# Attention over 32 graphs: xT loaded a batch ahead, keys in natural order, squares loaded in four transfers

## What is computed

```
q = x @ Wq.T ; k = x @ Wk.T ; v = x @ Wv.T + bv          # split into 12 heads
a = einsum('bnhd,bmhd->bhnm', q, k) * 384**-0.5 + adj[:, None]
a = where(all(a == 0, axis=-1), -inf, a) ; a = nan_to_num(softmax(a))
o = einsum('bhnm,bmhd->bnhd', a, v).reshape(B, N, 384)
y = layernorm(x + o @ Wo.T + bo)
```

## Time and profile before

| | |
|---|---|
| median of three runs | 781.46 us (780.7 to 782.91) |
| the profiled execution | 779.59 us, its span 777.70 us |
| busy: PE, DVE, ACT, POOL | 93%, 77%, 79%, 58% of the span |
| mean granted clock of TensorE | 0.97 |
| transfers | 193 MB, 71.0% of 16 engines' span in the one queue of SP |
| squares: stores and loads | 64 each, 1024 KB each |
| xt, xr, out | 32 each, 384 KB each |
| bias_sq, bias | 32 each, 256 KB each |

### The profile page before, as it was taken

The page is one execution under the profiler, slowest core; times in us unless marked ns, Lnnn a source line. Parts: engine busy times, 40 slices in busy tenths (PEclk is TensorE's granted clock), DMA queues, the critical chain, the costliest instruction groups (busy, mean ns, idle before and its releaser), DMA issues.

```text
span 777.7 us, 22949 instructions
## 1 busy us (share of the span) xinstructions
PE 722.7 (93%) x7480; PEld 613.3 (79%) x7480; DVE 594.9 (77%) x2216; ACT 615.1 (79%) x1991; POOL 453.2 (58%) x518
## 2 busy tenths in 40 slices
PE   7788999999999899999999999999999999998753
PEld 6777888888888788888888888888888888876632
DVE  2776887888887788888788888888788888878821
ACT  2786888888888788898888888988889889878711
POOL 3425666765666676656666756566667665665321
PEclk8999999999999999999999999999999999999955
DMA  8187768778777876878768778786787777776621
GB/s 256 55 283 233 257 236 283 246 262 299 253 259 235 278 260 249 301 263 280 261 244 294 259 246 294 264 284 231 268 290 268 249 286 270 247 279 233 248 81 42
DMA packets 92664, 193.00 MB, mean 248 GB/s; under 512 B 4736, under 2 KB 51584, under 8 KB 84352
## 3 DMA queue, kind: packets, MB, share of 16 engines
q1 hardware_dynamic: 92544, 191.52, 71.0%
HBM read 111.80 MB, written 79.69 MB: 246 GB/s over the span
## 4 chain that ended last, share of the span: by engine, by line
PE 61%; DMA 18%; POOL 7%; ACT 5%; issue 4%; DVE 2%; SPq 1%; POOLq 0%; ACTq 0%; DVEq 0%
PE bank_b L532 35%; DMA xt<-in_xT 14%; PE bank_a L619 8%; PE s_bank L578 7%; PE bank_t L589 6%; POOL xt_lo L323 4%; PE bank_c L532 4%; ACT prob L437 3%; PE bank_c L600 2%; POOL xt_hi L321 2%; ACT y_out L468 2%; DMA sq_dram<-w_f 2%; DVE neg L782 1%; DMA xr<-in_x 1%; SPq L259 1%
## 5 line engine op out<-in xcount | busy, mean ns | idle before, releaser
L437 ACT ACTIVATE prob<-neg,negmax 128x256 f32<-128x256 f32 x768 | 380.8, 501 | 37.6 <-DVE negmax L782 35.1
L782 DVE CUSTOM_DVE_ANT_0 neg<-s_bank,bias_sq 128x256 f32<-128x256 f32 x512 | 191.0, 410 | 47.0 <-PE s_bank L578 46.1
L796 DVE STREAM_TRANSPOSE w_f<-prob 128x512 f32<-128x512 f32 x256 | 173.1, 695 | 0.0
L437 ACT ACTIVATION_READ_ACCUMULATOR prob<-neg,negmax 128x1 f32 x768 | 148.1, 193 | 0.0
L532 PE MATMUL bank_b<-xt_hi,w_hi 128*128 128x256 f32 x384 | 117.1, 305 | 20.1 <-POOL xt_lo L323 16.4
L334 POOL TENSOR_TENSOR kq_lo<-kq,kq_hi 128x512 fp32r<-128x512 f32 x96 | 124.0, 1291 | 7.7
L532 PE MATMUL bank_b<-xt_lo,w_hi 128*128 128x256 f32 x384 | 110.7, 288 | 0.0
L532 PE MATMUL bank_b<-xt_hi,w_lo 128*128 128x256 f32 x384 | 110.4, 288 | 0.0
L782 DVE CUSTOM_DVE_ANT_0 neg<-s_bank,bias 128x256 f32<-128x256 f32 x256 | 92.3, 416 | 10.6 <-PE s_bank L578 10.5
L532 PEld LDWEIGHTS bank_b<-xt_hi,w_hi 128*128 128x128 f32 x384 | 75.1, 196 | 30.1 <-issue 20.0
L360 POOL TENSOR_SCALAR var_eps<-meanvar 128x2 f32<-128x2 f32 x32 | 7.3, 227 | 151.4 <-DVE meanvar L880 151.4
(11 more groups left out here) (66 smaller groups left out, 1835.6 us busy)
## 6 DMA issues: line engine op xcount, KB each, us to landing
sq_dram<-w_f SPq DMA_DIRECT2D x64, 1024.0 KB, 5.9
sq_probT<-sq_dram SPq DMA_DIRECT2D x64, 1024.0 KB, 5.9
xt<-in_xT SPq DMA_DIRECT2D x32, 384.0 KB, 5.9
xr<-in_x SPq DMA_DIRECT2D x32, 384.0 KB, 4.6
out_y<-y_out SPq DMA_DIRECT2D x32, 384.0 KB, 5.1
bias_sq<-in_adjP SPq DMA_DIRECT2D x32, 256.0 KB, 6.2
bias<-in_adj SPq DMA_DIRECT2D x32, 256.0 KB, 6.1
w_f<-in_wkT SPq DMA_DIRECT2D x3, 192.0 KB, 3.9
```

What stands on the lines that cost most here:

```text
L437: nc.scalar.activation(prob[:, u % PROB_RING, k], neg[:, h, w.c], ACT.Exp, scale=-1.0, bias=negmax[t.p][:, w.c, h:h + 1], accum_out=sums[t ...
L782: nc.vector.tensor_tensor_reduce(out=neg[:, h, w.c], in0=s_bank[h % JH][:, w.c, :], in1=by[t.p][:, w.c, :], scale=-1.0, scalar=BIG, op0=AL ...
L796: nc.vector.transpose(sq_stage[w.g][:, :, a:a + PAIR, :, w.c].rearrange("p b h m s -> p (h m) b s"), prob[:, u % PROB_RING].rearrange("p k ...
```

## The change

SP's step is reordered, one input goes, and the keys keep their natural order.

- xt of batch t+3 is loaded in step t, between the store and the load of squares 0. It was xt of t+2 at the start of the step. The loops start one step sooner for it (-3 instead of -2).
- `bias_sq` and `adjP` are gone. `bias` serves all three groups and is loaded for t+2, where bias_sq was.
- `load_squares` issues four transfers, one for each block b: partitions 32b to 32b+31 get the 32 rows of that block, again in pieces of 2 KB. The added wait is in the count: `sq_loaded` goes up by 64 instead of 16, and those who wait on it (SP ahead of the next store, PE ahead of `weigh`) wait for the four.
- ACT copies K01 as it copies the two other pieces, by the line that was L420.

```diff
 def steps(body):
-    for c in range(-2, 34):
+    for c in range(-3, 34):
...
-            def load_bias_sq(t):
-                after(sp, neg_ready, t.count(H * NT, -H * NT))
-                sp.dma_start(bias_sq[t.p][:], adjP[t.c].rearrange("(c p) m -> p c m", p=P)
-                             ).then_inc(bias_sq_loaded[t.p], DMA)
...
-                after(sp, sq_loaded[g], t.count(DMA))
+                after(sp, sq_loaded[g], t.count(BLOCKS * DMA))
...
-                sp.dma_start(sq_probT[g][:].rearrange("p i h m c s -> p i (h m c s)"),
-                             sq_dram[g].rearrange("(i r) b n -> (r b) i n", i=BLOCKS)).then_inc(sq_loaded[g], DMA)
+                for b in range(BLOCKS):
+                    sp.dma_start(sq_probT[g][SQ * b:SQ * (b + 1)].rearrange("p i h m c s -> p i (h m c s)"),
+                                 sq_dram[g][:, b, :].rearrange("(i r) n -> r i n", i=BLOCKS)
+                                 ).then_inc(sq_loaded[g], DMA)
...
             def step(t):
+                nxt3 = t.later(3)
                 nxt2 = t.later(2)
-                nxt = t.later(1)
                 prev2 = t.later(-2)
-                if nxt2.alive and nxt2.c >= 2:
-                    load_xt(nxt2)
-                if nxt.alive and not nxt.first:
-                    load_bias(nxt)
                 if t.alive:
                     store_squares(t, 0)
+                if nxt3.alive and nxt3.c >= 2:
+                    load_xt(nxt3)
+                if t.alive:
                     load_squares(t, 0)
                     store_squares(t, 1)
                     load_xr(t)
                     load_squares(t, 1)
                 if nxt2.alive and not nxt2.first:
-                    load_bias_sq(nxt2)
+                    load_bias(nxt2)
...
-                if name == "K01":
-
-                    nc.scalar.activation(kq[:, 0:2, :].rearrange("p a (m b r) -> p (a m) r b", m=NT, b=BLOCKS),
-                                         bank[name][:].rearrange("p (a m r b) -> p (a m) r b", a=2, m=NT, b=BLOCKS),
-                                         ACT.Copy).then_inc(kq_saved[name], 1)
-                else:
-                    nc.scalar.activation(kq[:, a:a + 2, :], bank[name][:].rearrange("p (a n) -> p a n", a=2),
-                                         ACT.Copy).then_inc(kq_saved[name], 1)
+                nc.scalar.activation(kq[:, a:a + 2, :], bank[name][:].rearrange("p (a n) -> p a n", a=2),
+                                     ACT.Copy).then_inc(kq_saved[name], 1)
...
-                    pe.wait_ge(sq_loaded[g], t.count(DMA, DMA))
+                    pe.wait_ge(sq_loaded[g], t.count(BLOCKS * DMA, BLOCKS * DMA))
...
-                by = bias_sq if w.g < SQUARED else bias
                 for h in w.heads:
                     nc.vector.tensor_tensor_reduce(out=neg[:, h, w.c], in0=s_bank[h % JH][:, w.c, :],
-                                                   in1=by[t.p][:, w.c, :], scale=-1.0, scalar=BIG,
+                                                   in1=bias[t.p][:, w.c, :], scale=-1.0, scalar=BIG,
```

More of the change, by code:

```diff
@@ L80, in steps, with build @@
 def steps(body):
-    for c in range(-2, 34):
+    for c in range(-3, 34):
         body(Batch(c))
-def build(nc, x, xT, adj, adjP, wqT, wkT, wvT, bv, woT, bo, out):
+def build(nc, x, xT, adj, wqT, wkT, wvT, bv, woT, bo, out):
     def sb(name, shape, dt=F32):
@@ L101, in build @@
     bias = [sb(f"bias{p}", [P, NT, N]) for p in range(2)]
-    bias_sq = [sb(f"bias_sq{p}", [P, NT, N]) for p in range(2)]
     kq = sb("kq", [P, 2 * KC, N])
@@ L164, in build @@
     bias_loaded = [sem(f"bias_loaded{p}") for p in range(2)]
-    bias_sq_loaded = [sem(f"bias_sq_loaded{p}") for p in range(2)]
     xt_hi_ready = sem("xt_hi_ready")
@@ L270, in _ @@
             load_w(W_Q, wqT)
-            load_bias_sq(Batch(0))
+            load_bias(Batch(0))
             load_xt(Batch(1))
@@ L274, in _ @@
             load_b(bv_all, bv)
-            load_bias(Batch(0))
             load_b(bo_all, bo)
@@ L773, in add_bias @@
                 if u == 0:
-                    dve.wait_ge(bias_sq_loaded[t.p], t.loads())
-                if u == TURNED:
                     dve.wait_ge(bias_loaded[t.p], t.loads())
@@ L936, in _ @@
             steps(step)
-_INS = ["x", "xT", "adj", "adjP", "wqT", "wkT", "wvT", "bv", "woT", "bo"]
+_INS = ["x", "xT", "adj", "wqT", "wkT", "wvT", "bv", "woT", "bo"]
 def kernel(x, adj, L0_gnn_Wq, L0_gnn_Wk, L0_gnn_Wv, L0_gnn_bv, L0_gnn_Wo, L0_gnn_bo):
@@ L945 @@
     from concourse.bass_utils import run_bass_kernel_spmd
-    adjP = np.asarray(adj).reshape(B, N, NT, SQ, BLOCKS).transpose(0, 1, 2, 4, 3).reshape(B, N, N)
     arrays = {
-        "x": np.asarray(x), "xT": np.asarray(x).transpose(0, 2, 1), "adj": np.asarray(adj), "adjP": adjP,
+        "x": np.asarray(x), "xT": np.asarray(x).transpose(0, 2, 1), "adj": np.asarray(adj),
         "wqT": np.asarray(L0_gnn_Wq).T, "wkT": np.asarray(L0_gnn_Wk).T, "wvT": np.asarray(L0_gnn_Wv).T,
```

## The result

The changed kernel takes 796.37 us, the median of four runs (793.93 to 803.72), against 781.08 us for the kernel before in its four. The ratio is 1.0223, with a 95% interval of 1.0173 to 1.0273: slower by 2.2%. The forecast was 768.1 us and faster; rival (a), at 800, is what happened. The profiled execution took 793.93 us, with a span of 792.0.

The account below looks back on a forecast made before the run. The prediction took PE to bound the kernel, at 21.85 us a batch, plus waits for xt. 779.59 - 15.8 + 1.2 + 1.2 = 766.2 us for the profiled execution, 768.1 in the median; range 761 to 803 us.

Parts of the forecast that it names:

- rival (a): Slower: quarter transfers of squares run at about half rate and the DMA chain becomes the bound; 800 us, chance 0.33.
- What bounded the kernel before: PE, with 21.85 us of its own time a batch; waits for xt_lo added 16.4 us over the run.
- xt's part: Loading xt a batch sooner ends POOL's wait for it and nearly all of PE's for xt_lo: gain 15.8 us.
- xt in the hole: xt's 1.0 us transfer fits the 2.5 us lull between group 0's store and load: no cost in steady state.
- K01's copy and the single bias at 0: ACT's copy, 1101 to 599 ns, runs beside PE's work; nobody waits for the bias load: both 0 us.
- The count of transfers: Three more issues per group on SP's queue, 1.2 us: hidden except at the start and last batch, 1.2 us each.
- The slack of the chain, 3.75 us: Room in the store-load chain: idle 2.0 us plus 1.9 freed by moving xt and dropping a bias, less 0.15.
- x: Extra time per load of squares from 32-partition transfers: 0, 2.1 or 2.7 us; taken below the threshold of 1.9.
- The rate of a transfer into 32 partitions: Loads of squares: untested by the trace, bounded by 388 and 194 GB/s; chosen fast enough to lose nothing.
- the rule that the prediction quotes from the Trainium skill: 32 partitions reach half of the ports: 189 GB/s for 1 MiB against 328 for 128, or 2.3 us more per load.
- the prediction's own formula: Above the threshold of 1.9 us, the batch takes 21.85 + 2x - 3.75 us; below it nothing is lost.
- The landing check: Squares of both groups, 1.2 us later, still land before PE uses them, with 2 us or more left.

Follow-up runs that it names:

- xt_only: The kernel before with only xt's load moved, a batch sooner, between store and load of squares 0: 763.0 us, ratio 0.978.
- after_no_xt: The changed kernel without xt's transfers from batch 2 on (12 MB less, wrong output): 797.3 us, ratio 1.018.
- xt_part: xt_only with both groups' loads of squares as four transfers of 32 partitions each, permuted layout kept: 792.5 us, ratio 1.014.
- by_rows: The kernel before with each load of squares as four transfers, each a quarter of the row to all 128 partitions: 784.2 us, ratio 1.004.
- delay_g0: xt_only plus one tiny 8 KB transfer, waited for, before group 0's load of squares: 809.0 us, ratio 1.033.
- delay_g1: xt_only plus the same tiny transfer and wait, before group 1's load instead: 797.4 us, ratio 1.017.
- xt_part_g1: xt_only with only group 1's load as four transfers of 32 partitions, group 0's staying one of 128: 777.5 us, ratio 0.992.
- after_reorder: The changed kernel with bias and out_y issued behind store 0 of the next step, not ahead of it: 792.6 us, ratio 1.012.

## Why the prediction was wrong

**What bounded the kernel before, and xt's part: right.** Batches without the wait take 21.85 us, xt_only shows nearly all of them, and its 763.0 us is a little under the 765.7 that the sum gives for it.

**xt in the hole: right**, for the changed kernel, by after_no_xt.

**K01's copy and the single bias at 0: not contradicted for the copy, true of the bias only while PE is the bound.** The copy fell from 1101 to 582 ns, and no run times it alone. The bias in front of a store is worth 0.5 us a batch once the round of transfers is the bound; that nobody waits for it holds only while PE is. xt_part against the changed kernel doesn't show that gain, and the stamps say what stands against it: store 0 does land 0.7 us sooner in the changed kernel (5.9 for 6.6), but its load 0 takes 0.7 us longer to PE's first use (8.0 for 7.3, means over all batches). Whether that comes of the order in which its transfers take the rows stays open.

**The count of transfers: nearly right.** by_rows loses 0.4% (0.1 to 0.8), 3 us, where the sum had 2.4.

**The slack of the chain, 3.75 us: mis-sized, and this is the step that failed.** The prediction let the batch grow only by what 2x has above 3.75 us, and so nothing be lost up to x = 1.9. delay_g0 tests the slack without a slow load. By the same count xt_only has 3.0 us of it (2.0 idle, 0.39 MB at 340 GB/s = 1.15 freed, less 0.15). A delay of 2.1 us should have cost nothing; it cost 1.3, and in delay_g1 1.9 cost 1.2. So the spare room was 0.6 to 0.8 us and not 3.0. In the changed kernel, 21.2 less the bias's 0.5 leaves a round of 20.7 and a slack of 1.2 where the sum had 3.75; this is an estimate, by the reading of the round above.

Two faults may make the 2.6 us; both are argued only. The stretches were read in one batch, 282.96 to 304.80, chosen because nothing waited in it, and it was a fast one: load 0 at 3.96 us where the mean of its kernel is 4.45, load 1 8.20 us behind load 0 where the mean is 9.01, 1.3 us in all. And taking xt and bias out of a busy stretch was priced at that stretch's mean rate, as if the rest would move up, but part of the rest was waiting for its own landing.

**The rate of a transfer into 32 partitions: taken at the wrong end.** The bounds 388 and 194 GB/s held the 210 measured, and the rule that the prediction quotes from the Trainium skill, page "SBUF — State Buffer", section "Door 1: The DMA port swizzle", named the mechanism. "I take x below the threshold" was made by the nearness of one row, 220 GB/s, which belongs to transfers of another kind. Measured alone, x is 2.25 us in the data and 1.65 to the landing, as small transfers start to flow sooner; that reason was right. In the changed kernel the data of load 0 flow at 222 GB/s, 4.7 us for 2.7 (x = 2.0), and its landing comes some 1.7 us later than that of one transfer (8.2 for 6.5). So x lay at the threshold of 1.9, and couldn't decide by itself: with x = 2.0 the prediction's own formula gives 21.85 + 4.0 - 3.75 = 22.1 us a batch, and some 776 us. The other 0.7 us a batch, up to 22.8, is the slack's.

How the two share the loss isn't settled. By the round of 20.7 the batch pays (22.8 - 20.7) / 2 = 1.05 us for each slow load, less than it is longer by. xt_part_g1 agrees, 21.2 + 1.05 = 22.3 against 22.27; xt_part doesn't, 23.3 against 22.76.

**The landing check was made from the wrong landing.** "Both have 2 us or more left" used 3.96 us for store 0. In the changed kernel the store lands after 5.9 us, as load 1, the bias and out_y of the step before are still ahead of it (with the last two behind it, in after_reorder, it lands after 4.8). That is the same round seen from PE: 5.9 + 8.0 for the quarter loads + 8.8 = 22.7 us.

**The rivals.** (a) came with the signs named for it: 222 GB/s at share 1.02, waits on the squares in most batches, the batch at 22.8. Its price at 800 was near partly by luck: it took x as 2.7, too large, and a slack of 3.75, too large as well. I gave it 0.33 where the rule quoted from the Trainium skill and the lack of any row for a partial transfer should have given it more than the forecast.

## What to carry to other kernels

Where a store to DRAM and its load back are chained by waits, the chain can bound the kernel with the DMA engines 0.76 busy. Its slack is better measured, by adding a tiny transfer and a wait, than summed from idle shares, least of all those of a batch picked for being undisturbed. A transfer behind a store and ahead of the load that waits for it was free here (0.39 MB, in two places), while 0.26 MB ahead of a store cost 0.5 us a batch. Four loads into a quarter of the partitions each are no substitute for one into all: price a split by what partitions it reaches, and not by how many issues it takes.

The version that beats both is xt_only, 763.0 us: the xT part alone, with the permuted layout kept.

## What the runs showed of the hardware

A load that stays within partitions 0 to 63 or within 64 to 127 moved about 210 GB/s, one into all 128 moved 382. Between 32 and 64 partitions it is the side and not the number that counts: 512 KB into 64 partitions took 5.1 to 5.2 us on one side and 3.9 to 4.0 across both. Alternating the sides from one transfer to the next in one queue did little (6.7 us for 1 MB, 6.9 in order), and two queues helped little (239 GB/s against 228). The share of the DMA engines reads 1.0 in both cases, so it doesn't tell a slow transfer from a fast one; the GB/s beside it does. And a transfer behind another in the queue did not delay that one's landing: without xt behind it store 0 landed after 6.1 us, with it after 5.9.
